# Moving weight preparation and operand splits to other places in a fused attention and three-adapter kernel

## The reference, cut to what matters

```
q, k, v = x @ Wq, x @ Wk, x @ Wv
attn_out = softmax(q k^T * 512**-0.5) v @ Wp + bp
cms_out  = gelu(attn_out @ cW1 + cb1) @ cW2 + cb2 + one_hot(code)       # 512 -> 2048 -> 512
modifier = gelu(concat(attn_out, cms_out) @ mW1 + mb1) @ mW2 + mb2      # 1024 -> 2048 -> 512
y0 = clip(x + cms_out + modifier, 0, 1)
three times: h = gelu(y @ Wd[e] + bd[e]) @ Wu[e] + bu[e]; y = layernorm(y + h) * g[e] + b[e]
```

## Time and profile before

| | before |
|---|---|
| median of 3 runs | 1236.32 us (1235.46 to 1237.9) |
| profiled execution | 1239.01 us |
| its span (first to last instruction) | 1236.9 us |
| mean granted TensorE clock | 0.994 of 2.4 GHz |
| PE busy | 1191.9 us, 96% |
| PE weight loads (beside PE) | 973.7 us, 79% |
| DVE busy | 807.4 us, 65% |
| ACT busy | 567.0 us, 46% |
| POOL busy | 173.5 us, 14% |
| largest share of the chain that ended last | PE 71%, DVE 11%, POOL 8% |

### The profile page before, as it was taken

How to read it: one execution, slowest core, us unless ns; L and a number is a source line. 1 busy time by engine, 2 the same in 40 slices (tenths; PEclk the granted TensorE clock), 3 DMA queues, 4 the chain that set the end, 5 groups by cost and what they waited for, 6 DMA issues and landing times.

```text
span 1236.9 us, 15228 instructions
## 1 busy us (share of the span) xinstructions
PE 1191.9 (96%) x5312; PEld 973.7 (79%) x5312; DVE 807.4 (65%) x1461; ACT 567.0 (46%) x1068; POOL 173.5 (14%) x147
## 2 busy tenths in 40 slices
PE   7999999799999899999999999989999999999997
PEld 5878878677788688888887787768888888788776
DVE  5444385746766766565766666686665565879986
ACT  5334353554533534343524633544343433266666
POOL 1332230000000000000000000000000000488871
PEclk9999999899999999999999999999999999999999
DMA  5755452114312202020461221411111118655534
GB/s 189 271 199 180 162 176 85 43 43 153 122 58 77 87 16 94 10 94 9 169 274 51 88 83 51 171 51 51 52 52 52 52 34 322 229 189 193 175 137 170
DMA packets 51186, 145.82 MB, mean 118 GB/s; under 512 B 6420, under 2 KB 6420, under 8 KB 46886
## 3 DMA queue, kind: packets, MB, share of 16 engines
q1 hardware_dynamic: 51110, 144.84, 33.2%
HBM read 108.11 MB, written 36.71 MB: 117 GB/s over the span
## 4 chain that ended last, share of the span: by engine, by line
PE 71%; DVE 11%; POOL 8%; ACT 4%; issue 4%; DMA 1%; SPq 0%; POOLq 0%; DVEq 0%; ACTq 0%
PE psum L541 70%; POOL res L1525 3%; POOL res L1527 3%; DVE ring L1187 1%; DMA prep<-wdu_dram 1%; ACT z L1016 1%; ACT ring L877 1%; POOL sm L1518 1%; DVE g_hl L1254 1%; DVE sm L1434 1%; DVE res L1269 1%; DVE res L1324 1%; DVE w_t L1228 0%; DMA wk_raw<-wts_dram 0%; POOL prep L1498 0%
## 5 line engine op out<-in xcount | busy, mean ns | idle before, releaser
L541 PE MATMUL psum<-g_hl,w_hl 128*128 128x512 f32 x1536 | 353.3, 390 | 1.5 <-DVE g L1242 1.3
L541 PE MATMUL psum<-a_op,ring 128*128 128x512 f32 x1344 | 324.4, 394 | 17.5 <-DVE w_t L1228 11.1
L541 PEld LDWEIGHTS psum<-g_hl,w_hl 128*128 128x128 f32 x1536 | 287.9, 188 | 64.6 <-DVE g L1242 4.8
L541 PEld LDWEIGHTS psum<-a_op,ring 128*128 128x128 f32 x1344 | 252.9, 190 | 77.8 <-DVE w_t L1228 14.5
L541 PE MATMUL psum<-c_op,ring 128*128 128x512 f32 x672 | 166.1, 394 | 0.6 <-DVE c_op L1296 0.6
L1254 DVE TENSOR_TENSOR g_hl<-g,g_hl 128x512 fp32r<-128x512 f32 x128 | 87.7, 691 | 111.7 <-ACT g_hl L917 110.4
L541 PEld LDWEIGHTS psum<-c_op,ring 128*128 128x128 f32 x672 | 127.3, 190 | 28.5 <-DVE c_op L1296 2.0
L1506 POOL TENSOR_TENSOR yT<-res,yT 128x512 fp32r<-128x512 f32 x8 | 11.7, 1487 | 875.6 <-ACT yT L1011 875.6
L877 ACT CAST ring<-asum 128x256 fp32r<-128x256 f32 x192 | 76.2, 403 | 122.3 <-PE psum L541 100.9
L917 ACT CAST g_hl<-g 128x512 fp32r<-128x512 f32 x128 | 78.3, 618 | 101.1 <-PE psum L541 101.1
L1187 DVE TENSOR_TENSOR ring<-asum,ring 128x256 fp32r<-128x256 f32 x192 | 80.8, 422 | 63.8 <-ACT ring L877 61.3
(11 more groups left out here) (124 smaller groups left out, 1381.2 us busy)
## 6 DMA issues: line engine op xcount, KB each, us to landing
rawp<-up_w_dram SPq DMA_DIRECT2D x48, 512.0 KB, 3.6
wdu_split<-prep SPq DMA_DIRECT2D x36, 512.0 KB, 2.9
wraw<-dn_w_dram SPq DMA_DIRECT2D x64, 256.0 KB, 3.1
wd<-wdu_split SPq DMA_DIRECT2D x12, 1024.0 KB, 7.3
wu<-wdu_split SPq DMA_DIRECT2D x12, 1024.0 KB, 5.4
prep<-wdu_dram SPq DMA_DIRECT2D x36, 256.0 KB, 3.3
second_pair_operands<-c_op SPq DMA_DIRECT2D x7, 1024.0 KB, 6.9
a_op<-second_pair_operands SPq DMA_DIRECT2D x7, 1024.0 KB, 11.3
```

Of the source, the lines that this page charges most:

```text
L541: ins = nc.tensor.matmul(ps, lw(el), rw(er), start=first and i == 0, stop=last and i == 2, skip_group_check=skip)
```

## The change

`SUMS_AT` keeps only the sums of the second quad's pieces (in quad 0). The sums of the next chunk's first quad and its first five weight operands, which stood in quad 1, are made in steps 0 to 5 of the down projection. In chunk 0 the splits and sums of P7, P5, P6 and P4 are put later, some of them in the down projection (`DOWN`). In chunks 4 and 12 the splits of P2, P4, P3 and the sum of P4 get places of their own (`LAYER_SUM`, `LAYER_HI`, `LAYER_LO`) in place of one split at each of places 0 to 6. The work on y0 in chunks 8 and 9 goes to the down steps. No instruction is added or removed.

```diff
--- before.py
+++ after.py
@@ -344,13 +344,21 @@
         U_AT, V_AT, W_AT, C22_AT, C21_AT = (1, 5), (2, 8), (3, 8), (4, 9), (6, 12)
         G12_AT, G22_AT, G11_AT, G21_AT = (1, 1), (5, 10), (5, 11), (6, 13)
 
-        SUMS_AT = ((1, 2, 3), (4, 5, 6)), ((8, 9, 10), (11, 12, 13))
+
+        SUMS_AT = ((1, 2, 3),), ((8, 9, 10), (11, 12, 13))
+        SUMS_DOWN = (0, 1, 3), (2, 4, 5)
 
         PRE_AT = ((2, 3, 4, 5, 6), (4, 6, 8, 10, 12))
         C22, C11, C21, C12 = range(4)
-        SECOND_PAIR_SUM = {(0, 3): P7, (0, 6): P5, (1, 2): P6, (1, 5): P4}
-        SECOND_PAIR_HI = {(0, 1): P3, (0, 4): P7, (0, 6): P5, (1, 3): P6, (1, 5): P4}
-        SECOND_PAIR_LO = {(0, 2): P3, (0, 5): P7, (1, 0): P5, (1, 4): P6, (1, 6): P4}
+
+
+        DOWN = QC
+        SECOND_PAIR_SUM = {(0, 5): P7, (1, 5): P5, (DOWN, 1): P6, (DOWN, 4): P4}
+        SECOND_PAIR_HI = {(0, 1): P3, (0, 6): P7, (1, 6): P5, (DOWN, 2): P6, (DOWN, 5): P4}
+        SECOND_PAIR_LO = {(0, 3): P3, (1, 1): P7, (DOWN, 0): P5, (DOWN, 3): P6, (DOWN, 6): P4}
+        LAYER_SUM = {1: P6, 7: P4}
+        LAYER_HI = {0: P7, 1: P5, 2: P6, 5: P2, 7: P4, 9: P3}
+        LAYER_LO = {1: P7, 2: P5, 3: P6, 6: P2, 8: P4, 10: P3}
 
         A_ORDER = (P1, P3, P2, P7, P5, P6, P4), (P1, P2, P3, P7, P5, P6, P4)
         C_ORDER = (P1, P7, P5, P6, P2, P4, P3)
@@ -981,11 +989,9 @@
                             gelu(ci, q, C21)
                         if ci == 0 and (q, pos) in SECOND_PAIR_HI:
                             second_pair_hi(SECOND_PAIR_HI[q, pos])
-                        if ci == NCHUNK + 1 and pos in (2, 4):
-                            first_pair_y0_hi(q, (2, 4).index(pos))
-                        if ci % NCHUNK == 4 and q == 0 and pos < PROD - 1:
-                            layer_hi(p, C_ORDER[pos + 1])
-                        if n + AHEAD < PAIRS * AOP:
+                        if ci % NCHUNK == 4 and q == 0 and pos in LAYER_HI:
+                            layer_hi(p, LAYER_HI[pos])
+                        if n + AHEAD < aop_at(ci, 0) + QC * len(LAYER_STEPS[l]):
                             weight_hi(n + AHEAD)
                         if q == 1 and pos in PRE_AT[l]:
                             at_ = PRE_AT[l].index(pos)
@@ -1000,6 +1006,12 @@
                         g_hi(ci, d + 2)
                     if d in (2, 4):
                         down_weight_hi(ci, d // 2 + 1)
+                    if d < AHEAD and ci + 1 < NCH:
+                        weight_hi(aop_at(ci + 1, 0) + d)
+                    if ci == 0 and (DOWN, d) in SECOND_PAIR_HI:
+                        second_pair_hi(SECOND_PAIR_HI[DOWN, d])
+                    if ci == NCHUNK + 1 and d < 2 * PAIRS:
+                        first_pair_y0_hi(d // 2, d % 2)
                 if ci % NCHUNK == 4 - 1:
                     layer_hi(p, P1)
                 if ci % NCHUNK == 0:
@@ -1204,16 +1216,15 @@
                         dve.wait_ge(sums_done, 4 * n + 3)
                         nc.vector.tensor_tensor(dst[:, 3, :], src[:, 1, :], dst[:, 1, :], ALU.subtract).then_inc(sums_done, 1)
 
-            def next_sums(ci, q, pos):
-
-                ni, nq = (ci, 1) if q == 0 else (ci + 1, 0)
-                if ni == NCH:
-                    return
-                piece = piece_at(ni, nq)
-                l, nl = chunk_of(ci)[1], chunk_of(ni)[1]
-                for part, places in enumerate(SUMS_AT[l][:nl + 1]):
+            def second_quad_sums(ci, pos):
+                for part, places in enumerate(SUMS_AT[chunk_of(ci)[1]]):
                     if pos in places:
-                        weight_sums(piece + part, ((0, 1), (2,), (3,))[places.index(pos)])
+                        weight_sums(piece_at(ci, 1) + part, ((0, 1), (2,), (3,))[places.index(pos)])
+
+            def next_chunk_sums(ci, d):
+                for part, places in enumerate(SUMS_DOWN[:chunk_of(ci)[1] + 1]):
+                    if d in places:
+                        weight_sums(piece_at(ci, 0) + part, ((0, 1), (2,), (3,))[places.index(d)])
 
             def combine_v(ci, q):
                 Q = QC * ci + q
@@ -1347,22 +1358,17 @@
                             attention_sum(1, SECOND_PAIR_SUM[q, pos])
                         if ci == 0 and (q, pos) in SECOND_PAIR_LO:
                             attention_lo(1, SECOND_PAIR_LO[q, pos])
-                        if ci == NCHUNK and pos in (0, 2, 4, 6):
-                            (y0_add, y0_clip)[pos // 2 % 2](q, pos // 4)
-                        if ci == NCHUNK + 1 and pos in (3, 5):
-                            first_pair_y0_lo(q, (3, 5).index(pos))
                         if ci % NCHUNK == 4 and q == 0 and pos == 0:
                             layer_sum(p, P7)
                             layer_sum(p, P5)
-                        if ci % NCHUNK == 4 and q == 0 and 1 <= pos < PROD:
-                            layer_lo(p, C_ORDER[pos])
-                        if ci % NCHUNK == 4 and q == 0 and pos == 1:
-                            layer_sum(p, P6)
-                        if ci % NCHUNK == 4 and q == 0 and pos == 3:
-                            layer_sum(p, P4)
-                        if n + AHEAD < PAIRS * AOP:
+                        if ci % NCHUNK == 4 and q == 0 and pos in LAYER_LO:
+                            layer_lo(p, LAYER_LO[pos])
+                        if ci % NCHUNK == 4 and q == 0 and pos in LAYER_SUM:
+                            layer_sum(p, LAYER_SUM[pos])
+                        if n + AHEAD < aop_at(ci, 0) + QC * len(LAYER_STEPS[l]):
                             weight_lo(n + AHEAD)
-                        next_sums(ci, q, pos)
+                        if q == 0:
+                            second_quad_sums(ci, pos)
                         if q == 1 and pos in PRE_AT[l]:
                             at_ = PRE_AT[l].index(pos)
                             if at_ in (0, 3):
@@ -1376,6 +1382,18 @@
                         g_lo(ci, d + 2)
                     if d in (2, 4):
                         down_weight_lo(ci, d // 2 + 1)
+                    if ci + 1 < NCH:
+                        next_chunk_sums(ci + 1, d)
+                    if d < AHEAD and ci + 1 < NCH:
+                        weight_lo(aop_at(ci + 1, 0) + d)
+                    if ci == 0 and (DOWN, d) in SECOND_PAIR_SUM:
+                        attention_sum(1, SECOND_PAIR_SUM[DOWN, d])
+                    if ci == 0 and (DOWN, d) in SECOND_PAIR_LO:
+                        attention_lo(1, SECOND_PAIR_LO[DOWN, d])
+                    if ci == NCHUNK:
+                        (y0_add, y0_clip)[d // 4](d % 4 // 2, d % 2)
+                    if ci == NCHUNK + 1 and 1 <= d <= 2 * PAIRS:
+                        first_pair_y0_lo((d - 1) // 2, (d - 1) % 2)
                     if ci == NCH - 1 and d in (2, 3):
                         x_add(d - 2)
                 if ci % NCHUNK == 4 - 1:
```

## The result

| | before | changed |
|---|---|---|
| median | 1237.11 us (4 runs, 1235.46 to 1239.85) | 1217.67 us (4 runs, 1216.56 to 1218.37) |
| ratio, changed to before | | 0.9834, 95% interval 0.9818 to 0.985 |
| profiled execution, its span | 1239.01, 1236.9 us | 1217.09, 1215.0 us |
| the sixteen chunks, from the traces | 839.0 us | 818.7 us |

The kernel became 1.7% faster; 1217.7 us had been forecast. The page of the changed kernel: its span, part 1 (busy time, share of the span, instructions) and the chain that ended last, by engine.

The account below looks back on a forecast made before the run. PE, busy 96% of the span, bounds the kernel; only its pauses, mostly waits for DVE, can be won. 4.6 + 5.4 + 6.2 + 2.4 = 18.6 us off 1236.3 gives 1217.7, range 1212 to 1224.

Parts of the forecast that it names:

- The bound of 34.2 us: Sixteen loop chunks: 839.0 us taken against 804.8 needed with PE always busy, so 34.2 us is all that can be won.
- Part 1: Chunks 1, 2, 3, 10, 11: next chunk's preparation moves to the down projection, clearing both small pauses; 4.6 us gained.
- the serial chain: Down projection: a step's ACT and DVE work runs without overlap, 2.55 us, under the step's 2.72, so nothing accumulates.
- Part 2: Chunks 8 and 9: y0 work leaves the quads for the down steps; 5.4 us gained.
- The 0.3 us set aside: Chunks 8 and 9: 0.3 us taken as lost in both together, DVE load reaching 3.0 us in down steps 0 to 4.
- Part 3: Chunk 0: second pair's sums and splits go later; 52.1 us falls to 45.9, a gain of 6.2 (5.4 to 7.0).
- the half clock loss: Chunk 0: half of one 1.7 us clock loss, 0.8 us, counted because a 2.4 us pause lies between known cases.
- Part 4: Boundary chunks 4 and 12: splits and P4's sum go later; 1.2 us each, 2.4 us for both.
- the exchange of one wait for another: Chunks 4 and 12: 1.6 us won at place 8 mostly becomes a longer w pause before place 10; 0.86 kept.
- A: Chunks 4 and 12: v and w aren't held, only 0.6 us pauses and no clock loss remain; 8.6 more, 1209; 7%.
- B: Chunk 0 and boundaries: each pause is traded for another of the same length; only 10.0 us gained, 1226; 12%.
- C: Down projection, steps 1 to 4: handovers make it late, 2.2 us in each of 15 chunks, 33 us, 1251; 3%.

Follow-up runs that it names:

- part 1 alone: Kernel before with only the next chunk's sums and first five weight operands moved to the down projection: 1226.56 us, ratio 0.9929.
- the extra instructions: Changed kernel with 1 to 5 unused DVE additions in each of down steps 0 to 4 of chunks 1, 2, 3, 10, 11: 1240.6 us.
- early-gelu runs: One single-column gelu added on ACT ahead of the loop, in the kernel before (1236.66 us) and in the changed kernel (1216.58 us).
- the swap: Changed kernel with P3's weight copy ahead of P4's high half on ACT, place 7, first quad of chunks 4 and 12: 1213.38 us, ratio 0.982.
- the version above: Changed kernel with the swap, sixth weight operand in the down projection, P3's boundary low half earlier, chunk 0's splits and sums re-placed: 1210.18 us, ratio 0.9778.
- part 4 undone: Changed kernel with the splits and P4's sum of chunks 4 and 12 back at the places of the kernel before: 1219.23 us.

## Why the prediction came out right

**Where time is lost.** The bound of 34.2 us, and the chunks it lies in, held: no chunk changed that had no pause.

The sum was made by chunk, and so are these comparisons. What each edit gives by itself differs: 11.3 of the 20.5 us come with part 1 alone.

**Part 1**, forecast 4.6, measured 4.7. L1234 and L1242 (by their lines before) are in time in every plain layer-0 chunk, and no pause came up in the down projection. The safety margin was worked out in a wrong way (the serial chain; the extra instructions show more room), which did no harm here.

**Part 2**, forecast 5.4, measured 5.7. The 0.3 us set aside for down steps over 2.72 us of load weren't needed: PE is busy all through both chunks. Most of this gain is part 1's, which also leaves these quads; alone it brings chunks 8 and 9 to 41.0 and 42.1 us.

**Part 3**, forecast 6.2, measured 8.1: the term that was mis-sized. The step that failed reads "ACT's table load of 1.28 us stays, about 1.1 us earlier, and holds the copies behind it", with the load ending at 227.2, behind L1234. In the trace it starts at 221.50, as soon as ACT has nothing else, and the gelu follows L1234 by 0.04 us (223.78). In the trace before it had started at 227.23, which was when ACT came free and not when the input came. With it off the path, what stands behind is about 1.3 us earlier: place 5 of quad 1 loses 1.2 us with its restart instead of 2.7. The early-gelu runs show both halves of this. The other 0.8 is the half clock loss that was counted and didn't come. 45.9 - 1.3 - 0.8 = 43.8, measured 44.0. The other two losses were near: about 0.9 before place 6 (forecast 0.8) and 1.1 in the down projection (forecast 0.8), for L1253 and the third down weight.

**Part 4**, forecast 2.4, measured 2.0. The order was walked rightly, to 0.1 us at place 10, and the exchange of one wait for another is shown by the swap. What differs is how often the clock fell: twice in this execution (65.1 and 64.9, forecast 65.1 with a fall), not at all in the early-gelu one (63.9 each, which is the 66.0 before less 2.1). But 2.1 compares a fall with none: the order of the kernel before takes 64.4 where the clock stays up, so 0.5 of it is the edit's and 1.6 the clock's.

The sum was 18.6; the loop gave 20.5 in the profiled executions and the medians 19.4, beside a median before that was 0.8 us higher (1237.11) than the one predicted from. So that the forecast hit to 0.1 us is luck: the sum was 1.9 us too small for the loop, nearly all of it in chunk 0, and the medians happened to differ by less than the profiled executions (21.9 us, of which 2.2 lie ahead of the loop). Executions of one kernel differ by that much: four of the kernel before span 4.4 us, and with the same order of work a boundary chunk takes 66.0 us in one trace and 64.4 in another, as the clock falls or not. The steps are right to about 2 us, not to 0.1.

**The rivals.** A (the boundary clears, 60.5 us a chunk) didn't happen; the swap gets to 62.4 and the version above to 61.4. B is out for chunk 0, where 5.7 us come on top of part 1, but close for the boundary, where only 0.5 us a chunk is left at equal clock. C is out, with two instructions of room in each step of a layer-0 chunk.

**What stays open.** The clock after a boundary pause. With the order of the kernel before, and the same pauses, it fell in both chunks (before), in chunk 12 only (part 1 alone, and the early gelu in the kernel before) or in none (part 4 undone). With the changed order it fell in both (changed), in chunk 12 only (the loaded down projection) or in none (the early gelu in the changed kernel). No run made it fall or hold at will. Parts 2 and 3 weren't run by themselves; their shares are differences. The 2.2 us ahead of the loop weren't looked into.

## What to carry to other kernels

When one engine is nearly full and waits for another only at places, price each place by walking the late engine's own list from a row, instruction by instruction; counting busy time would have put DVE at 65% and found nothing. A move that clears one wait is worth only what the next reader on the same list leaves of it, so walk on to the end of the stretch. In two engines that feed each other, look at which item stands ahead of the copy that the other one's head waits for: one swap on ACT (1.5 us a chunk at equal clock) was worth more than the whole re-placing of the splits (0.5). And run an edit alone before a gain is put down to it: the work that left the quads with part 1 helped most chunks in which w was late.

## What the runs showed of the hardware

- The activation table load runs before the wait of the instruction it belongs to: it starts once ACT has finished the instruction ahead (221.50 us, with gelu's input at 223.74), and costs nothing where ACT would have idled for 1.28 us.
- POOL's instruction of 128 x 1024 with both inputs in SBUF takes 2.50 us, and a DVE instruction with two SBUF inputs beside it ends 2.2 us late (3.40 instead of 1.22). DVE additions with one input in PSUM, beside POOL, took no longer (two in 1.27 us).
- After the same pause of 2.6 us before place 10 the granted clock fell to 1.2 GHz in two chunks of one execution and in none of another's; a fall cost 1.2 and 1.0 us (65.1 and 64.9 against 63.9). With the pauses of 1.35 and 1.83 us of the kernel before it cost 1.6 (66.0 against 64.4).
